# Two seams of a four-layer network on one core: projections between the steps of the ternary feed-forward, and the second attention as one sequence of chunks

## The reference, cut to what matters

```
x = x + ln(attn0(ln(x)))   # 32 heads, scores of a token with its own keys only
x = x + ln(ffn0(ln(x)))    # sigmoid(x1) * x2, weights quantized to -1, 0, 1; 1408 hidden units
x = x + ln(attn1(ln(x)))   # below
x = x + ln(ffn1(ln(x)))    # silu(gate) * up, the 2 largest of 4 kept; 2048 hidden units
...
q = x @ q_w.T;  kv = x @ kv_w.T;  k, v = split(kv)      # 16 heads of 32, 4 heads of keys and values
q = rope(q);  k = rope(k)
logits = q k^T / sqrt(dk) + causal mask                 # 1024 x 1024 for each head and batch
out = softmax(logits) v;  return out @ c_w.T
```

## Time and profile before

| | us |
|---|---|
| median of 3 runs | 1474.61 |
| lowest and highest | 1469.93, 1476.92 |
| the profiled execution | 1471.07 |
| its span, first to last instruction | 1468.4 |
| PE busy in the span | 1365.8 (93%) |
| DVE, ACT, POOL busy | 1026.0, 652.8, 695.7 |
| mean granted clock of TensorE | 0.965 of full |

### The profile page before, as it was taken

How to read it: one execution, slowest core, us unless ns; L and a number is a source line. 1 busy time by engine, 2 the same in 40 slices (tenths; PEclk the granted TensorE clock), 3 DMA queues, 4 the chain that set the end, 5 groups by cost and what they waited for, 6 DMA issues and landing times.

```text
span 1468.4 us, 19654 instructions
## 1 busy us (share of the span) xinstructions
PE 1365.8 (93%) x7238; PEld 937.5 (64%) x7238; DVE 1026.0 (70%) x2122; ACT 652.8 (44%) x1142; POOL 695.7 (47%) x841
## 2 busy tenths in 40 slices
PE   6997999999897999999799998999999999999997
PEld 5984445444564444477444445878888888888885
DVE  5897555664675777678677775388776877887776
ACT  5664322221323445652245566454545544454442
POOL 2575120221431223554112247576768767865862
PEclk9998999999986999999599999999999999999998
DMA  9100100000081110108411201423223223433300
GB/s 346 42 1 1 72 29 1 0 1 29 29 232 42 45 26 20 59 29 245 114 25 21 73 30 49 181 98 131 87 87 143 87 87 106 152 116 114 115 29 29
DMA packets 45927, 114.77 MB, mean 78 GB/s; under 512 B 3334, under 2 KB 4360, under 8 KB 42248
## 3 DMA queue, kind: packets, MB, share of 16 engines
q1 hardware_dynamic: 44760, 112.21, 23.2%
q10 hardware_dynamic: 1072, 1.31, 0.3%
HBM read 92.28 MB, written 20.97 MB: 77 GB/s over the span
## 4 chain that ended last, share of the span: by engine, by line
PE 64%; DVE 19%; ACT 5%; DMA 3%; SPq 3%; POOL 3%; issue 2%; POOLq 0%; DVEq 0%; ACTq 0%
PE PS L1439 62%; DVE cm L497 4%; DVE SM L513 2%; SPq L364 2%; DVE PS L705 2%; DMA QG<-MT 1%; DVE SM L509 1%; PE PS L1448 1%; SPq L372 1%; POOL SM L1255 1%; DVE SM L503 1%; DVE hm L506 1%; DMA qs<-qm 1%; ACT EX L1082 1%; DMA rw<-in_L_ffn_w_up 1%
## 5 line engine op out<-in xcount | busy, mean ns | idle before, releaser
L1082 ACT ACTIVATE EX<-PS 128x512 f32<-128x512 f32 (+3 forms) x384 | 167.3, 495 | 185.2 <-PE PS L1439 184.2
L1255 POOL TENSOR_TENSOR SM<-SM 128x1 f32<-128x1 f32 x256 | 109.6, 432 | 282.3 <-DVE SM L503 272.1
L1255 POOL TENSOR_TENSOR ws_g<-rw,ws_g 128x512 fp32r<-128x512 f32 x64 | 138.2, 2159 | 128.7 <-ACT ws_g L909 128.7
L1352 POOL TENSOR_SCALAR_AFFINE_SELECT EX<-EX 128x128 f32<-128x128 f32 x256 | 73.7, 299 | 242.0 <-ACT EX L1082 237.7
L1439 PE MATMUL PS<-KG,QG 96*128 96x512 f32 (+3 forms) x384 | 149.5, 427 | 15.5 <-DVE SM L705 11.9
L705 DVE CUSTOM_DVE_ANT_0 PS<-PS,MW 128x128 f32<-128x128 f32 (+3 forms) x256 | 121.7, 503 | 52.4 <-PE PS L1439 51.9
L1439 PE MATMUL PS<-QG,KG 98*128 98x512 f32 (+3 forms) x384 | 133.6, 389 | 19.2 <-DMA QG<-MT 17.2
L1224 ACT ACTIVATE ab<-hm 128x512 f32<-128x512 f32 x64 | 40.5, 633 | 204.5 <-DVE hm L497 204.5
L1439 PEld LDWEIGHTS PS<-QG,KG 98*128 98x128 f32 x384 | 72.5, 199 | 87.1 <-issue 47.8
L1439 PE MATMUL PS<-ws_d,HH 128*128 128x512 f32 x528 | 125.7, 389 | 0.2 <-DVE HH L497 0.2
L497 DVE TENSOR_TENSOR cm<-cm 128x512 bf16<-128x512 bf16 (+1 forms) x136 | 117.2, 892 | 2.4
(11 more groups left out here) (159 smaller groups left out, 2847.6 us busy)
## 6 DMA issues: line engine op xcount, KB each, us to landing
rw<-in_L_ffn_w_gate SPq DMA_DIRECT2D x16, 1024.0 KB, 5.1
rw<-in_L_ffn_w_up SPq DMA_DIRECT2D x16, 1024.0 KB, 5.1
...
```

The lines of the kernel that those rows point to most:

```text
L1082: e.activation(EX[:, n % 16, 0:W], PS[:, score_bank(n), 0:W], ACT.Exp, scale=ISQ, bias=0.0).then_inc(S["ex"], 1)
L1255: return e.tensor_tensor(out, a, b, op)
L1352: e.affine_select(out=p, in_=p, compare_op=ALU.is_ge, fill=0.0, base=0, pattern=[[1, 128]], channel_multiplier=-1).then_inc(S["sel"], 1)
```

## The change

Work of the second attention that stood between its parts is spread over what stands ahead of it.

- **Between the steps of the ternary feed-forward.** The 12 products of each batch become 6 units of two (a unit is two halves of a rotation, `whole(y)`, 24 matmuls; y = 3h + r, h the half batch). Units 0 to 8, the values of h = 0, 1, 2 (`value(h)`), the transposes of tiles 0 to 11, 16 maxima and the first turned maxima stand behind chosen steps (`extra`, and `between` the two halves of a step). All go through banks 6 and 7 with the old list; a bank is free when the item two back is evicted (`freed`). The weight transposes `jobs` move to steps 10 to 16 and 21 to 23. `turn_x` stands behind `up2`, no longer ahead of it. The norm tiles `xn` and `yn` of blocks 1 to 3 share a buffer, for which `norm2` waits until all of the first attention's sums are made.
- **One attention of 384 chunks**, 8 groups, with no loop over batches. Units 9, 10 and 11, the values of h = 3 and tiles 12 to 15 stand behind chunks 17 to 112, in the list of banks 0 to 2, where an item waits for the eviction of the one three back; `early` is gone: 32 maxima of group 0 stand behind chunks 2 to 12, three to a chunk. The maxima of group 4 (batch 1) stand behind chunks of group 3.
- **The output projection of batch 0** becomes 8 tiles behind chunks 218, 227, ... 281 (`proj_at`), copied out of the bank by ACT (`pc`). That of batch 1 stays behind the last chunk, where the sparse feed-forward's first transposes stand as before.
- **Banks.** Banks 0 to 3 hold the last down products when the chunks start: `scores` from chunk 2 on, and every item of banks 0 to 2, wait for the last norm `yn2` of `post2(3)`.
- **Transfers.** `unit_out` writes a unit as soon as it is split, `k_in` reads the keys of one group at a time, and all of x is kept in `xs` (8 tiles more than before).

```
+        jobs = {10 + c: ("q", c) for c in range(4)}
+        jobs.update({14: ("k", 0), 15: ("v", 0), 16: ("c", 0), 21: ("c", 1), 22: ("c", 2), 23: ("c", 3)})
...
+        for n, more in ((16, [("t3", 0), ("t3", 1)]), (17, [("t3", 2), ("t3", 3)]), (18, whole(0)), (20, whole(1)),
+                        (22, whole(2)), (24, value(0)), (25, [("VT", 0)]), (26, [("t3", 4), ("t3", 5)]),
+                        (27, [("t3", 6), ("t3", 7)]), (28, whole(3)), (29, whole(4)), (30, whole(5)), (31, value(1)),
+                        (32, [("VT", 1)]), (37, [("m", x) for x in range(2)] + [("t3", 8), ("t3", 9)]),
...
+            extra[n] = more
...
-        early = [[("m", 2 * v), ("m", 2 * v + 1)] for v in range(8)] + [[("h", 0)] + [("m", n) for n in range(16, 24)]]
         behind = [[] for _ in range(NS)]
-        for n in range(24):
-            behind[n // 2].append(("m", 24 + n))
+        for n in range(32):
+            behind[2 + n // 3].append(("m", 16 + n))
         behind[13].append(("h", 1))
-        for g in range(3):
+        behind[1].append(("VT", 2))
+        for n, i in ((17, 12), (18, 13), (24, 14), (25, 15)):
+            behind[n].append(("t3", i))
+        for n, y in ((57, 9), (61, 10), (105, 11)):
+            for x, t in enumerate(whole(y)):
+                behind[n + x].append(t)
+        for n, t in zip((109, 110, 112), value(3) + [("VT", 3)]):
+            behind[n].append(t)
+        proj_at = [218 + 9 * i for i in range(8)]
+        for i, n in enumerate(proj_at):
+            behind[n] += [("p", i, 0), ("p", i, 1)]
+        for g in range(7):
...
+        def freed(t):
+
+            x = misc_no[t] - 2 if t in misc_no else top_no[t] - 3
+            if x < 0:
+                return ("yn2", 16) if t in top_no else ("pr", NT)
...
-                    w.wait_ge(S["tpm"], misc_no[("x", i - 4)] + 1)
+                    w.wait_ge(S["tpm"], turned_no[("x", i - 4)] + 1)
+                    w.wait_ge(S["x1"], NT)
...
+            def projected(i):
+
+                w.wait_ge(S["ep"], i + 1)
+                w.wait_ge(S["en"], max(0, i - 1))
+                w.wait_ge(S["mv6"], max(0, i - 1))
+                cp(pc[:, i % 2, :], PS[:, bank3(("p", i)), :]).then_inc(S["pc"], 1)
...
-            for b in range(2):
-                for r in range(3):
-                    rope(b, r)
-                attention(b)
-                for step in range(12):
-                    project(b, step)
+            attention()
+            for step in range(12):
+                project(step)
...
-                w.wait_ge(S["ex"], NS * b + max(0, n - 2 if n < 163 else n - 5))
+                w.wait_ge(S["sg"], 44)
+                w.wait_ge(S["hd"], 44)
+                w.wait_ge(S["yn2"], 16 if n >= 2 else 0)
+
+                w.wait_ge(S["ex"], max(0, n - 2 if n < 355 else n - 5))
```

1128 lines of the change are left out of this document (598 added, 530 removed).

## The result

The changed kernel takes 1476.88 us (median of 8 runs, 1474.58 to 1480.19), the kernel before 1472.12 in the same session (8 runs, 1469.93 to 1476.92). The ratio is 1.003, 95% interval 1.0015 to 1.0044: no change by the bound of 0.5% that the prediction set, and a little slower rather than faster. The forecast was 1446, with a range of 1428 to 1466 and 0.88 on faster. It was wrong.

What follows compares the result with a forecast made beforehand. PE's own work was taken as the bound, except latency at the two batch entries. Terms 74.1 + 32.5 + 381.8 = 488.4 against 517.2, 28.8 us less: 1442.3 for the profiled execution, 1446 as median, range 1428 to 1466.

Steps and rivals of the forecast that it cites:

- Part 1: Ternary feed-forward: it gets longer by 74.1 us (66 to 76), 66.2 of inserted work and 7.9 of new waits.
- The rotation's waits: Ternary feed-forward: four items wait 0.8 us each for a unit's bank while DVE rotates, 3.3 us in all.
- the list of waits: Ternary feed-forward: new waits of 7.9 us, from rotations (3.3), maxima in steps 37 to 41 (3.5) and a later sigmoid (1.1).
- Part 2: New entry, last down product to chunk 16: 32.5 us, with bounds of 29 and 41.
- DVE becomes the bound: New entry: DVE's maxima, statistics and last reductions take 22.1 us, against about 14 for PE at the low clock.
- Part 3: Chunks from 16 on: 381.8 us (365 to 395), from 336.6 + 43.2 + 9.4 - 7.4.
- I let half of 14.8 be filled: Four groups that get products: half of PE's 14.8 us of idle time takes inserted work, -7.4 us.
- over 3 us a tile: Groups with output tiles: a cost above this per tile was named as a sign that the prediction is wrong.
- ACT's hold behind units 9 and 11: Among the chunks: exponentials wait in ACT's queue behind a unit's split, so PE loses 2.2 us at each.
- PE has room: Rival, chunks: PE absorbs all 43.2 us of inserted products, total 1410 us; chance 0.03.
- ACT's queue behind the output tiles: Rival, output tiles: each costs 3.3 us beside its product, and units the full 5.5 each, total 1481; chance 0.07.
- The clock stays low after the entry: Rival, after the entry: 1 to 4 us lost, or 16 to 28 if low through group 0 (1462 and more); chance 0.09.

Runs made afterwards that it cites:

- allin: `three` plus the edits of `entryshort`, `bankfree` and `actlater`: 1446.64 us, ratio 0.9816.
- three: The changed kernel with the edits of `memset34`, `maxfirst` and `cturns` together: 1462.92 us, ratio 0.9935.
- bankfree: `three` with a unit's banks freed by the last product that reads them, not by the sum behind it: 1460.77 us, ratio 0.9912.
- cturns: The changed kernel with the last projection weight's turned pieces in steps 19, 21, 23, 24, not 16, 21, 22, 23: 1470.24 us, ratio 0.9989.
- memset34: The changed kernel with POOL's memset of KG rows in step 34, not 38: 1472.5 us, ratio 1.0003.
- maxfirst: The changed kernel with DVE's maxima of steps 39 to 41 ahead of the step's own three operations: 1474.75 us, ratio 1.0011.
- entryshort: `three` with the last block's statistics behind the entry's maxima on DVE, and the last two maxima ahead of PE's first weighing: 1462.77 us, ratio 0.993.
- tiles2: The changed kernel with batch 0's eight output tiles at chunks where no maxima are asked for: 1475.41 us, ratio 1.0022.
- actlater: `three` with ACT's casts and POOL's subtractions of units 9 to 11 two chunks later: 1463.45 us, ratio 0.9919.

## Why the prediction was wrong, by its own steps

**Part 1, 74.1 forecast, 90.2 measured.** The inserted work, 66.2, was right within a few us: up to chunk 0 PE is busy for 413.48 us in `allin`, 67.0 more than the 346.45 of the kernel before, and with the edits of `three` and `bankfree`, which take waits away and no work, chunk 0 starts at 448.8, 72.4 behind 376.4. The rotation's waits (3.3 forecast, 0.75 + 0.75 + 1.02 + 0.75 measured) and their cause, the sum beside POOL, were right. The step that failed is the list of waits, 7.9 in all:
- The turned pieces of the last weight were not on it. I had counted their work and not their place behind three or four statistics in DVE's queue: 2.77 + 1.93 us (`cturns`).
- The memset of KG's two rows on POOL was counted at nothing. It held DVE's cast, and the maxima behind it, for 2.5 us (`memset34`).
- The maxima were put at 3.5 and cost 7.8 in the five steps, 2.80 of them by the memset. I had reckoned DVE free 2.1 us after down starts. In step 40 it is 2.4 (428.42 to 430.84), since the sigmoid stands behind the casts of the unit before in ACT's queue, and the wait is 1.16; step 41 is the same. The order in DVE's queue made these two waits (`maxfirst`). The bank of that unit costs 0.72 and 0.66 ahead of them.
- With them came low clocks at 285.1 and 401.1, 3.4 us each, not forecast at all.

**Part 2, 32.5 forecast, 36.4 measured.** "DVE becomes the bound" was right, as the stretch of the maxima and `entryshort` show, and "the clock hardly matters" too. The mark that I gave for it, DVE busy over nine tenths, was wrong: it is busy for 24.86 of 36.40, since the wait for `post2` at the start and the chain at the end hold no DVE work. The missing term is DVE's wait of 3.08 us for PE's first weighing ahead of the last two maxima. Of these about 1.3 are the low clock (3.2 - 1.9), an estimate, so it was not quite nothing.

**Part 3, 381.8 forecast, 397.1 measured.** By group (worked out from the forecast's terms, measured, in `allin`): group 0 35.3, 36.9, 37.5; group 1 59.9, 64.6, 59.8; group 2 53.6, 53.3, 52.4; group 3 44.6, 44.7, 44.6; groups 4 and 5 107.5, 116.6, 113.6; group 6 44.6, 45.2, 44.9; group 7 36.5, 35.8, 35.8.
- Group 1: the wait of 4.0 us was forecast and came (4.06). The 13.7 us of low clock behind it, which cost the 4.7, were not. In `allin` it was 6.8.
- Groups 4 and 5: the step that failed is "I let half of 14.8 be filled". Nothing was filled where the tiles stood, among the maxima. At a clock of 1.00 the two groups take 113.6 = 2 x 44.6 + 24.4, or 3.05 a tile against 2.74 of products. Of the 9.1 us that were missing, 3.7 are this half, 2.5 the 0.31 a tile above its products, and 3.0 came with the low clock of 6.8 us at 776.6. The mark "over 3 us a tile" spoke against me. Away from the maxima a tile took 2.5 (`tiles2`), so a little idle time can be filled, but not there.
- ACT's hold behind units 9 and 11 (2.2 each) was put too high; `actlater` finds 1 in all. In groups 1 and 2 this offset the idle time that wasn't filled.

**Rivals.** "PE has room", for which the share of weight loads spoke, is out: groups 4 and 5 were busy with matmuls for 103.91 of 113.60 us at 53% of weight loads, and took the products in full and a little more. The matmul rows were the better guide here. "ACT's queue behind the output tiles" wanted 3.3 us a tile beside its products; in the changed kernel it was 3.4 in all, low clock included. "The clock stays low after the entry" was partly right: it was low for 3.4 us at 500.1, for 13.7 at 568.4 and for 6.8 at 776.6, but not through group 0. None of the rivals was what happened: a dozen waits of 0.3 to 3 us that were not on the list, low clocks behind some of them, and 7.4 us of products that I had let idle time take.

**The sum.** `allin` does the same work in another order. It has 70.0 + 31.9 + 388.6 = 490.5 us for the path where 488.4 were forecast, and its median is near the 1446 of the forecast. That these meet is in part luck: `allin` is without some costs that the forecast had counted (3.3 of the rotation's waits, 4.3 of statistics ahead of the maxima), and it has others that the forecast had not. The terms of work were right. The waits are what a list of work doesn't hold.
